# Normalisations and statistics of neighbouring batches moved to other heads of a batch in an attention and expert kernel

## The chip, the cores and the metric

The kernel runs on one core of a Trainium2 chip. Its time is that of one execution on the device, in microseconds. The engines are TensorE (PE, with its weight loads as PEld), VectorE (DVE), ScalarE (ACT), GpSimd (POOL) and SyncE (SP, which only issues transfers). Each runs its own list of instructions in order and waits on semaphores for the others.

## What is computed

Tokens of 8 batches of 512 are embedded (width 256), then go through a causal attention with 8 heads of width 128 and rotary positions, and through a layer of 8 experts. Cut to what matters, with `_layernorm(x) = (x - mean) / sqrt(var + 1e-5)`:

```python
h = jnp.take(weight, x, axis=0)
h = h + attention(_layernorm(h, axis=-1), w_aq, w_ak, w_av, w_ao)
h = h + experts(_layernorm(h, axis=-1), Wr, W1, b1, W2, b2)
```

```python
q, k, v = einsum('btm,mhd->bthd', x, w_a*)
s = einsum('bihd,bjhd->bhij', _rope(q), _rope(k)) / D_HEAD - 1e30 * (i < j)
r = einsum('bihd,hdm->bim', softmax(s) @ v, w_ao)
```

The first layernorm is needed ahead of a batch's first head. The second needs the output of the batch's last head, and its result is wanted only by the experts, after all batches.

## The kernel before

The attention stage takes the span up to some 746 us, the router and the experts the rest; the change touches the attention alone. All products are in fp32 split into a high and a low part: `x_hi` is made by ACT (L254), `x_lo` by DVE or POOL (L354, L218), and each product is three matmuls (L546).

The loop is written out by hand (`batches`, L107): for each batch `b`, eight slots, `h` = 0 to 7, and three more at the end of the last batch. Slot `h` does four heads at once in a pipeline, on every engine in a fixed order:

- head `h`: projections of q and k, the rotation, a block of the values;
- head `h-1`: scores in four row blocks (`minimum` on DVE L411, `exp` on ACT L272), and POOL's first three normalisations (`norm`, L198) at the end of the slot;
- head `h-2`: the last normalisation, transposes of the probabilities on TensorE in three fills (`turn`, L600), their high parts on ACT and low parts on DVE (`t_low`);
- head `h-3`: probabilities by values (`weigh`) and output projection (`output`).

POOL's order in a slot is: `q_sin` (L206, after DVE's `rope_q` L387 and ACT's swap L295), `q_cos` (L212), `norm` of head `h-2`'s last block, `k_cos` (L212), `qT_lo` and `kT_lo` (L218), then the extras of the slot, then `norm` of head `h-1` after DVE's `inverse` (L418), then further extras. ACT makes `qT_hi` after `q_cos`, then `exp 0`, then `v_hi`. DVE makes `rope_q`, `turn_k` (L395 to L397), `oT_lo`, `t_low 0`, `minimum 0, 1, 2`, extras, `v_lo`, extras, `t_low 1`, `minimum 3`, `t_low 2`, `inverse`, extras. TensorE starts a slot with the projection of q, which waits for the previous slot's last `v_lo`, since both use the bank `proj_ps[0]`; `turn 0` waits for two of the normalisations at the end of the slot before, `turn 1` for the last block's, `weigh` for `t_low 1` and, in its last part, for `t_low 2` of the slot before.

The extras are the work of neighbouring batches:

- for batch `b+1`: four gathers of embedding rows by POOL (`gather`, L171: block 0 in slot 3, block 1 in slot 4, blocks 2 and 3 in slot 5), `stats_of` (L360) and `aggregate` (L366) on DVE in slot 6, the root on POOL (`rsqrt`, L178 and L181) in slot 6 ahead of `norm`, `normalise` (L374) on DVE at the end of slot 6, the transposes `xt` (L555) on TensorE in slot 7, and their high and low parts `xT_hi`, `xT_lo`;
- for batch `b-1`: `evacuate` at the end of slot 2, `stats2_of` (L436) in slot 3, `aggregate2` (L443) at its end, the root `rsqrt2` (L187, L190) on POOL at the end of slot 4, and `normalise2` (L451) in slot 5, two blocks ahead of `v_lo` and two ahead of `t_low 1`.

In batch 0 there is no work for a batch before, in batch 7 none for a batch after.

Of the kernel before, what the change touches and what calls it, by code (L numbers as in the profile page):

```python
# [14 lines left out]
H, D = 8, 128  # L15
VOCAB = 8000
N = B * T
TB = T // P
# [20 lines left out]
def build_attention(nc, a, ident, h2, x2, wr, shared):  # L39
# [3 lines left out]
    with ctx:  # L43
# [117 lines left out]
        def _(pool):  # L161
# [3 lines left out]
            def gather(b, blocks):  # L165
                after(pool, "ids_in", (b + 1) * 16)
                after(pool, "res_in", b * 16)
                after(pool, "xn_ready", b)
                alone(pool)
                for tb in blocks:  # L170
                    pool.indirect_dma_start(emb[:, tb, :], None, a["emb"][:, :],  # L171
                                            bass.IndirectOffsetOnAxis(ids[:, tb:tb + 1], 0))\
                        .then_inc(s["emb_in"], 16)

            def rsqrt(b):
                after(pool, "aggr_done", b + 1)
                alone(pool)
                nc.gpsimd.tensor_scalar(rstd[:], mean_var[:, :, 1], EPS, None, ALU.add)\  # L178
                    .then_inc(s["var_eps"], 1)
                after(pool, "var_eps", b + 1)  # L180
                nc.gpsimd.tensor_tensor(rstd[:], rstd[:], neg_half[:], ALU.pow)\  # L181
                    .then_inc(s["rstd_done"], 1)
# [42 lines left out]
            def body(b, slots, ok):  # L225
                for h in slots:
                    n = b * H + h
                    live = ok(h) and h < H
                    if live:
                        add(b, h, "q")  # L230
                    if ok(h - 2):
                        after(pool, "inv_done", 2 * (n - 2) + 2)
                        norm(b, h - 2, [3])
                    if live:
                        add(b, h, "k")
                        low(b, h, "q")
                        low(b, h, "k")
                    if len(slots) == H and h in (3, 4, 5):
                        gather(b + 1, [h - 3])
                    if len(slots) == H and h == 6:  # L240
                        rsqrt(b + 1)
                    if ok(h - 1):
                        after(pool, "inv_done", 2 * (n - 1) + 1)
                        norm(b, h - 1, [0, 1, 2])
                    if len(slots) == H and h == 5:
                        gather(b + 1, [3])
                    if h == 4 and not (isinstance(b, int) and b == 0):
                        rsqrt2(b - 1)
            batches(pool, body)

        @block.scalar
# [100 lines left out]
        def _(dve):  # L352
# [13 lines left out]
                    last = nc.vector.bn_aggr(mean_var[:, tb, :], stats[:, tb, :])  # L366
                last.then_inc(s["aggr_done"], 1)

            def normalise(b):
                after(dve, "rstd_done", b + 1)  # L370
                after(dve, "h2_out", 16 * (b - 1))
                after(dve, "xt_tr", KT * b)
                for tb in range(TB):
                    last = nc.vector.tensor_scalar(xn[:, tb, :], emb[:, tb, :], mean_var[:, tb, 0:1],  # L374
                                                   rstd[:, tb:tb + 1], ALU.subtract, ALU.mult)
                last.then_inc(s["xn_ready"], 1)

            def xt(b):
                for kt in range(KT):
# [76 lines left out]
            def layernorm2(b, h, half):  # L456


                if isinstance(b, int) and b == 0 or h >= H:
                    return  # L460
                if h == 3:
                    stats2_of(b - 1, range(2 * half, 2 * half + 2))
                if h == 5:
                    normalise2(b - 1, range(2 * half, 2 * half + 2))

            dve.wait_ge(s["mask_ready"], 2)
            stats_of(0, range(TB))
            aggregate(0)
            normalise(0)
            after(dve, "w_hi", 1)  # L470
            low_of(w_qkv["q"][1][:], wraw["q"], w_qkv["q"][0][:], "w_lo")
            xt(0)
# [5 lines left out]
            def body(b, slots, ok):  # L478
                for h in slots:
# [14 lines left out]
                    if ok(h - 1):  # L494
# [3 lines left out]
                        after(dve, "s_done", 3 * (n - 1) + 2)  # L498
                        minimum(b, h - 1, 1)
                        minimum(b, h - 1, 2)  # L500
                    layernorm2(b, h, 0)
                    if len(slots) == H and h == 6:
                        stats_of(b + 1, [0, 1])
                    if live:
                        for i, t in enumerate(V_SLOT[h]):
                            after(dve, "v_hi", 2 * TB * b + t + 1)
                            low_of(v[1][:, t, :], proj_ps[i][:], v[0][:, t, :], "v_lo")
                    if isinstance(b, int) and b == 0 and h == 1:
                        after(dve, "w_hi", 4)
                        low_of(w_o[1][:], wraw_o, w_o[0][:], "w_lo")  # L510
                    if len(slots) == H and h == 7:
                        xt(b + 1)
                    layernorm2(b, h, 1)
                    if len(slots) == H and h == 6:
                        stats_of(b + 1, [2, 3])
                        aggregate(b + 1)
                    if ok(h - 2):
                        t_low(b, h - 2, 1)
                    if ok(h - 1):
                        after(dve, "s_done", 3 * (n - 1) + 3)  # L520
                        minimum(b, h - 1, 3)
# [8 lines left out]
                        aggregate2(b - 1)  # L530
                    if h == 10:
                        evacuate(b)
                    if len(slots) == H and h == 6:
                        normalise(b + 1)
            batches(dve, body)

        @block.tensor
# [921 lines left out]
```

## Time and profile before

| | before |
|---|---|
| median of 3 runs | 1239.88 us (1239.66 to 1241.63) |
| the profiled execution | 1239.33 us |
| its span, first to last instruction | 1237.4 us |
| PE busy | 1121.4 us (91%) |
| DVE busy | 830.0 us (67%) |
| POOL busy | 819.0 us (66%) |
| ACT busy | 692.1 us (56%) |
| mean granted clock of TensorE | 0.970 of full speed |

The page gives the busy time of each engine, and then shows the span in slices and the costliest groups. In a timeline a row is one instruction, or several alike that follow each other (x2, x3): its start from the beginning of the span, its length, engine, line, operation, the tiles (written <- read), and in brackets how long the engine was idle before it and what ended that. The tile `h` at L374 is `xn`, `x` at L451 is `x2`, and all PSUM tiles are called `bank`. A slot is here the stretch from TensorE's first matmul of one head's projection to that of the next.

### The profile page before, as it was taken

How to read it: one execution, taken by the hardware profiler on the slowest of the kernel's cores; microseconds unless marked ns; L12 is line 12 of the kernel's file. 1: busy time of each engine (PE TensorE's matmuls, PEld its weight loads, DVE VectorE, ACT ScalarE, POOL GpSimd, SP SyncE). 2: the span in 40 equal slices, each digit the busy share in tenths (PEclk: the TensorE clock that was granted, in tenths of full speed). 3: DMA queues.
4: the chain of work that ended last, by engine and by line, in shares of the span. 5: the costliest groups of instructions: out<-in, count | busy, mean ns of one | idle time of the engine just before them, and what ended most of it. 6: DMA issues, size and time to landing. Idle time of an engine off the chain costs nothing. (4 is left out here: it accounts for less than half of the span.)

```text
span 1237.4 us, 19984 instructions
## 1 busy us (share of the span) xinstructions
PE 1121.4 (91%) x6999; PEld 982.0 (79%) x6999; DVE 830.0 (67%) x1964; ACT 692.1 (56%) x1434; POOL 819.0 (66%) x886
## 2 busy tenths in 40 slices
PE   3899999999999999999999998117999999999997
PEld 2788888888888878878888874016999999999996
DVE  4777787887787787887887855774554555554433
ACT  3666666656656666666666654004554654655542
POOL 3797897887887888887987851014664654744534
PEclk9999999999999999999999999558999999999999
DMA  5000110110100100100100003302433523624223
GB/s 191 1 18 1 39 31 1 39 30 2 44 26 1 44 26 1 44 27 3 46 22 35 18 1 108 107 13 57 121 81 67 129 38 101 134 35 108 26 26 34
DMA packets 42211, 58.09 MB, mean 47 GB/s; under 512 B 8897, under 2 KB 34945, under 8 KB 41985
## 3 DMA queue, kind: packets, MB, share of 16 engines
q0 software_dynamic: 13824, 21.24, 9.8%
q1 hardware_dynamic: 28288, 35.58, 8.7%
q8 instruction: 56, 0.92, 0.3%
q14 instruction: 43, 0.34, 0.1%
HBM read 35.71 MB, written 16.91 MB: 43 GB/s over the span
## 5 line engine op out<-in xcount | busy, mean ns | idle before, releaser
L1098 DVE TENSOR_TENSOR hT_lo<-hid,hT_hi 128x512 fp32r<-128x512 f32 x124 | 86.4, 697 | 170.1 <-ACT hT_hi L1245 157.2
L198 POOL TENSOR_SCALAR prob<-prob,row_inv 128x512 f32<-128x512 f32 (+3 forms) x256 | 135.3, 541 | 69.1 <-DVE row_inv L418 67.4
L1242 ACT ACTIVATE hid<-up,b_e 128x512 f32<-128x512 f32 x128 | 88.1, 688 | 150.4 <-PE up L1345 136.1
L272 ACT ACTIVATE prob<-prob,row_min 128x512 f32<-128x512 f32 (+3 forms) x256 | 142.4, 556 | 40.1 <-DVE row_min L411 39.3
L867 POOL DMA_INDIRECT x<-routed_rows,tokens x64 | 84.3, 1318 | 112.7 <-DVE tokens L1092 95.0
L354 DVE TENSOR_TENSOR pT_lo<-bank,pT_hi 128x384 fp32r<-128x384 f32 (+1 forms) x192 | 114.3, 595 | 42.4 <-ACT pT_hi L254 42.4
L878 POOL TENSOR_SCALAR y<-y,gate 128x256 f32<-128x256 f32 x60 | 32.4, 552 | 128.0 <-issue 127.2
L411 DVE CUSTOM_DVE_ANT_0 prob<-bank,mask_row 128x512 f32<-128x512 f32 (+3 forms) x256 | 114.1, 483 | 0.0
L206 POOL TENSOR_TENSOR q_sin<-q_sin,rope_t 128x512 f32<-128x512 f32 x64 | 82.5, 1290 | 43.6 <-ACT q_sin L296 42.0
L887 POOL DMA_INDIRECT out<-y,tokens x60 | 97.2, 1621 | 16.1 <-issue 13.9
L600 PE MATMUL bank<-ident,prob 128*128 128x128 f32 x640 | 101.7, 273 | 5.6 <-POOL prob L198 5.6
L254 ACT ACTIVATE pT_hi<-bank 128x384 fp32r<-128x384 f32 (+1 forms) x192 | 99.5, 518 | 2.7 <-PE bank L600 2.5
L218 POOL TENSOR_TENSOR kT_lo<-k_cos,kT_hi 128x512 fp32r<-128x512 f32 x64 | 83.0, 1296 | 9.6 <-ACT kT_hi L254 9.2
L212 POOL TENSOR_TENSOR q_cos<-q_cos,q_sin 128x512 f32<-128x512 f32 x64 | 82.6, 1291 | 5.0
L600 PEld LDWEIGHTS bank<-ident,prob 128*128 128x128 f32 x640 | 76.7, 140 | 10.8 <-POOL prob L198 8.5
L546 PE MATMUL bank<-pT_hi,v_hi 128*128 128x512 f32 (+3 forms) x256 | 83.2, 325 | 1.9 <-DVE pT_lo L354 1.9
L1245 ACT ACTIVATE hT_hi<-up,b_e 128x512 fp32r<-128x512 f32 x124 | 84.7, 683 | 0.0
L546 PE MATMUL bank<-kT_hi,qT_hi 128*128 128x512 f32 (+3 forms) x256 | 84.5, 330 | 0.0
L218 POOL TENSOR_TENSOR qT_lo<-q_cos,qT_hi 128x512 fp32r<-128x512 f32 x64 | 83.3, 1301 | 0.0
L546 PE MATMUL bank<-pT_hi,v_lo 128*128 128x512 f32 (+3 forms) x256 | 83.0, 324 | 0.0
L212 POOL TENSOR_TENSOR k_cos<-k_cos,k_sin 128x512 f32<-128x512 f32 x64 | 82.9, 1295 | 0.0
L546 PE MATMUL bank<-kT_hi,qT_lo 128*128 128x512 f32 (+3 forms) x256 | 82.7, 323 | 0.0
(239 smaller groups left out, 3821.7 us busy)
## 6 DMA issues: line engine op xcount, KB each, us to landing
raw<-in_w SPq DMA_DIRECT2D x16, 1024.0 KB
emb_res<-emb SPq DMA_DIRECT2D x8, 512.0 KB, 3.7
out<-h SPq DMA_DIRECT2D x8, 512.0 KB, 2.9
routed_rows<-x SPq DMA_DIRECT2D x8, 512.0 KB, 3.1
x<-in_wq SPq DMA_DIRECT2D x1, 1024.0 KB, 5.1
x<-in_wk SPq DMA_DIRECT2D x1, 1024.0 KB, 4.9
x<-in_wv SPq DMA_DIRECT2D x1, 1024.0 KB, 7.0
x<-in_wo SPq DMA_DIRECT2D x1, 1024.0 KB, 10.1
```

Source lines behind the costliest of these rows:

```text
L198: nc.gpsimd.tensor_scalar(pr, pr, row_inv[:, h % 2, k:k + 1], 1.0, ALU.mult, ALU.mult).then_inc(s["norm_done"], 1)
L212: nc.gpsimd.tensor_tensor(cos[:], cos[:], sin[:], ALU.add).then_inc(s[f"{x}_add"], 1)
L218: nc.gpsimd.tensor_tensor(out[1][:, h % 2, :], cos[:], out[0][:, h % 2, :].bitcast(F32), ALU.subtract).then_inc(s[f"{x}_lo"], 1)
L254: nc.scalar.activation(out, in_, ACT.Copy).then_inc(s[name], 1)
L272: nc.scalar.activation(pr, pr, ACT.Exp, bias=row_min[:, h % 2, k:k + 1], scale=-1.0, accum_out=row_sum[:, h % 2, k:k + 1]).then_inc(s["exp ...
L354: nc.vector.tensor_tensor(out, in_, hi.bitcast(F32), ALU.subtract)\
L411: nc.vector.tensor_tensor_reduce(prob[:, h % 2, col:col + w], s_ps[bk][:, pc:pc + w], mask_row[:, T - w:T], scale=-1.0 / D, scalar=3e38, o ...
L546: last = nc.tensor.matmul(out, l, r, start=start and c == 0, stop=stop and c == len(todo) - 1)
L600: last = nc.tensor.transpose(t_ps[f][:, c * P:(c + 1) * P], prob[:, h % 2, col:col + P], ident[:])
L887: pool.indirect_dma_start(a["out"][:, :], bass.IndirectOffsetOnAxis(tokens[e][:, TB * half + c:TB * half + c + 1], 0), y[half][:, c, :], N ...
L1098: nc.vector.tensor_tensor(out, in_, hi.bitcast(F32), ALU.subtract)\
L1242: nc.scalar.activation(hid[:, t % 2, :], up_ps[t % 2][:], ACT.Gelu, bias=bias)
```

## The change

- POOL: the gathers of blocks 0 and 1 stand in slot 3, those of blocks 2 and 3 in slot 4; none is left in slot 5. `rsqrt2(b - 1)` stands at the end of slot 3 instead of slot 4, and `rsqrt(b + 1)` at the end of slot 5 instead of in slot 6 ahead of `norm`.
- DVE: `v_lo` now stands ahead of the first half of the extras, and `t_low 1` ahead of the second half. `normalise2` is in slot 4 instead of 5; `stats_of` and `aggregate` are in slot 5 instead of 6; `normalise` takes a list of blocks and is cut in two halves within slot 6, in place of one piece at its end.
- No instruction is added or dropped, and no buffer changes.

```diff
--- before.py
+++ after.py
@@ -235,17 +235,15 @@
                         add(b, h, "k")
                         low(b, h, "q")
                         low(b, h, "k")
-                    if len(slots) == H and h in (3, 4, 5):
-                        gather(b + 1, [h - 3])
-                    if len(slots) == H and h == 6:
-                        rsqrt(b + 1)
+                    if len(slots) == H and h in (3, 4):
+                        gather(b + 1, [2 * h - 6, 2 * h - 5])
                     if ok(h - 1):
                         after(pool, "inv_done", 2 * (n - 1) + 1)
                         norm(b, h - 1, [0, 1, 2])
+                    if h == 3 and not (isinstance(b, int) and b == 0):
+                        rsqrt2(b - 1)
                     if len(slots) == H and h == 5:
-                        gather(b + 1, [3])
-                    if h == 4 and not (isinstance(b, int) and b == 0):
-                        rsqrt2(b - 1)
+                        rsqrt(b + 1)
             batches(pool, body)
 
         @block.scalar
@@ -366,14 +364,15 @@
                     last = nc.vector.bn_aggr(mean_var[:, tb, :], stats[:, tb, :])
                 last.then_inc(s["aggr_done"], 1)
 
-            def normalise(b):
+            def normalise(b, blocks):
                 after(dve, "rstd_done", b + 1)
                 after(dve, "h2_out", 16 * (b - 1))
                 after(dve, "xt_tr", KT * b)
-                for tb in range(TB):
+                for tb in blocks:
                     last = nc.vector.tensor_scalar(xn[:, tb, :], emb[:, tb, :], mean_var[:, tb, 0:1],
                                                    rstd[:, tb:tb + 1], ALU.subtract, ALU.mult)
-                last.then_inc(s["xn_ready"], 1)
+                if TB - 1 in blocks:
+                    last.then_inc(s["xn_ready"], 1)
 
             def xt(b):
                 for kt in range(KT):
@@ -460,13 +459,13 @@
                     return
                 if h == 3:
                     stats2_of(b - 1, range(2 * half, 2 * half + 2))
-                if h == 5:
+                if h == 4:
                     normalise2(b - 1, range(2 * half, 2 * half + 2))
 
             dve.wait_ge(s["mask_ready"], 2)
             stats_of(0, range(TB))
             aggregate(0)
-            normalise(0)
+            normalise(0, range(TB))
             after(dve, "w_hi", 1)
             low_of(w_qkv["q"][1][:], wraw["q"], w_qkv["q"][0][:], "w_lo")
             xt(0)
@@ -498,24 +497,28 @@
                         after(dve, "s_done", 3 * (n - 1) + 2)
                         minimum(b, h - 1, 1)
                         minimum(b, h - 1, 2)
-                    layernorm2(b, h, 0)
-                    if len(slots) == H and h == 6:
-                        stats_of(b + 1, [0, 1])
                     if live:
                         for i, t in enumerate(V_SLOT[h]):
                             after(dve, "v_hi", 2 * TB * b + t + 1)
                             low_of(v[1][:, t, :], proj_ps[i][:], v[0][:, t, :], "v_lo")
+                    layernorm2(b, h, 0)
+                    if len(slots) == H and h == 5:
+                        stats_of(b + 1, [0, 1])
+                    if len(slots) == H and h == 6:
+                        normalise(b + 1, [0, 1])
                     if isinstance(b, int) and b == 0 and h == 1:
                         after(dve, "w_hi", 4)
                         low_of(w_o[1][:], wraw_o, w_o[0][:], "w_lo")
                     if len(slots) == H and h == 7:
                         xt(b + 1)
+                    if ok(h - 2):
+                        t_low(b, h - 2, 1)
                     layernorm2(b, h, 1)
-                    if len(slots) == H and h == 6:
+                    if len(slots) == H and h == 5:
                         stats_of(b + 1, [2, 3])
                         aggregate(b + 1)
-                    if ok(h - 2):
-                        t_low(b, h - 2, 1)
+                    if len(slots) == H and h == 6:
+                        normalise(b + 1, [2, 3])
                     if ok(h - 1):
                         after(dve, "s_done", 3 * (n - 1) + 3)
                         minimum(b, h - 1, 3)
@@ -530,8 +533,6 @@
                         aggregate2(b - 1)
                     if h == 10:
                         evacuate(b)
-                    if len(slots) == H and h == 6:
-                        normalise(b + 1)
             batches(dve, body)
 
         @block.tensor
```

## Rows read from the trace of the kernel before

**Rows 1.** Busy time by stretch, slots 4 to 7 (length, engines' busy us, clock).

```profile
237.36:247.91 10.55, 10.55 (x68) 9.45 (x66) 7.74 (x25) 7.48 (x19) 10.16 (x11) 1.00 0.05 12
247.91:259.33 11.42, 10.79 (x67) 9.45 (x65) 10.18 (x22) 7.44 (x20) 10.70 (x13) 1.00 0.05 13
259.33:270.13 10.80, 10.80 (x65) 9.45 (x65) 9.04 (x24) 5.76 (x14) 9.43 (x11) 1.00 0.27 73
270.13:283.01 12.88, 11.12 (x68) 9.26 (x67) 10.83 (x30) 7.56 (x19) 10.48 (x13) 1.00 0.01 2
```

**Rows 2.** Timeline of TensorE, slots 5 to 7 (start, us, line, [idle before]).

```profile
252.70 0.49 PE L600 MATMUL bank<-ident,prob 128*128 128x128 f32 x3
...
259.33 0.50 PE L546 MATMUL bank<-xT_hi,wq_hi 128*128 128x512 f32 x1 [0.63 <-DVE v_lo L354]
...
280.29 0.66 PE L600 MATMUL bank<-ident,prob 128*128 128x128 f32 x4 [0.67 <-POOL prob L198]
...
283.01 0.50 PE L546 MATMUL bank<-xT_hi,wq_hi 128*128 128x512 f32 x1 [0.67 <-DVE xT_lo L354]
```

**Rows 3.** Waits, batches 1 to 6 (total us, times, longest).

```profile
PE bank L546 <- DVE v_lo L354: 3.8, 6, 0.6
```

**Rows 4.** Timeline of POOL, end of slot 3 to slot 5.

```profile
238.51 1.09 POOL L171 DMA_INDIRECT emb<-in_emb,ids  x1 [0.16 <-issue]
...
239.65 1.61 POOL L198 TENSOR_SCALAR prob<-prob,row_inv 128x512 f32<-128x512 f32 x3
...
241.37 1.29 POOL L206 TENSOR_TENSOR q_sin<-q_sin,rope_t 128x512 f32<-128x512 f32 x1
...
249.67 1.60 POOL L198 TENSOR_SCALAR prob<-prob,row_inv 128x512 f32<-128x512 f32 x3 [0.24 <-DVE row_inv L418]
...
252.74 1.29 POOL L206 TENSOR_TENSOR q_sin<-q_sin,rope_t 128x512 f32<-128x512 f32 x1
```

**Rows 5.** Timeline of POOL, kernel's start and batch 3's slot 3 (two pieces).

```profile
7.49 0.95 POOL L171 DMA_INDIRECT emb<-in_emb,ids  x1 [0.30 <-issue]
...
328.85 1.26 POOL L198 TENSOR_SCALAR prob<-prob,row_inv 128x512 f32<-128x512 f32 x2
```

**Rows 6.** Timelines, slot 6: the chain behind q_sin.

```profile
264.84 1.29 POOL L206 TENSOR_TENSOR q_sin<-q_sin,rope_t 128x512 f32<-128x512 f32 x1
...
269.38 0.69 DVE L354 TENSOR_TENSOR v_lo<-bank,v_hi 128x512 fp32r<-128x512 f32 x1 [1.27 <-ACT v_hi L254]
...
270.39 0.58 ACT L254 ACTIVATE pT_hi<-bank 128x512 fp32r<-128x512 f32 x1
```

**Rows 7.** Timelines, slots 5 and 6: normalisations and their company.

```profile
255.90 2.77 DVE L451 TENSOR_SCALAR x<-h,mean_var,rstd 128x256 f32<-128x256 f32 x2
...
257.19 1.34 POOL L218 TENSOR_TENSOR qT_lo<-q_cos,qT_hi 128x512 fp32r<-128x512 f32 x1
...
259.20 1.10 DVE L451 TENSOR_SCALAR x<-h,mean_var,rstd 128x256 f32<-128x256 f32 x2
...
273.21 2.02 DVE L374 TENSOR_SCALAR h<-emb,mean_var,rstd 128x256 f32<-128x256 f32 x4 [0.49 <-POOL rstd L181]
```

**Rows 8.** Timelines, ends of slots 5 and 6: statistics, t_low, inverse.

```profile
260.23 0.68 DVE L354 TENSOR_TENSOR pT_lo<-bank,pT_hi 128x512 fp32r<-128x512 f32 x1
...
261.64 0.16 DVE L418 RECIPROCAL row_inv<-row_sum 128x3 f32<-128x3 f32 x1
...
262.01 1.61 POOL L198 TENSOR_SCALAR prob<-prob,row_inv 128x512 f32<-128x512 f32 x3 [0.94 <-DVE row_inv L418]
...
269.99 0.74 DVE L360 BATCH_NORM_STATS2 stats<-emb 128x6 f32<-128x256 f32 x2
...
271.18 0.66 DVE L354 TENSOR_TENSOR pT_lo<-bank,pT_hi 128x512 fp32r<-128x512 f32 x1
```

**Rows 9.** Timelines, slot 7: rope_q and q_sin of head 7.

```profile
275.15 0.67 DVE L387 TENSOR_TENSOR q_cos<-bank,rope_t 128x512 f32<-128x512 f32 x1
...
277.14 1.28 POOL L206 TENSOR_TENSOR q_sin<-q_sin,rope_t 128x512 f32<-128x512 f32 x1 [2.05 <-ACT q_sin L296]
```

## The prediction

> **What bounds the kernel now.** I read four views in this order. First the busy times by stretch, cut where TensorE starts the projection of a new head (I call such a stretch a slot; batch 2 starts at 193.81 us) [rows 1]. In slot 4 TensorE is busy for all of its 10.55 us and DVE, ACT and POOL are not, so TensorE sets the pace; the clock is 1.00 throughout. Slots 5, 6 and 7 last 11.42, 10.80 and 12.88 us. Their matmuls are those of slot 4 (slot 7 has transposes of about the same length in place of one set of values), so 0.87 + 0.25 + about 2.3 = 3.4 us per batch is all that a better order could return, about 24 us over seven batches. Second, TensorE's own rows with a wait [rows 2]: slot 6 starts late because `v_lo` of slot 5 came late, slot 7's `turn 1` waits for POOL's `prob`, and slot 0 of the next batch waits for `xT_lo`. The first of these happens once in each of the batches 1 to 6 [rows 3]. Third, POOL and then DVE in order of time [rows 4, 6, 7, 8], because each of these late tiles comes out of POOL's or DVE's hand-written queue.
>
> The relation that I use most: POOL's `q_sin` of a head feeds `q_cos`, then ACT makes `qT_hi`, the first exponential and `v_hi`, and DVE makes `v_lo`, for which the next slot's projection waits. In slot 6 nothing in that chain waits for anything else: `q_sin` starts at 264.84, `v_lo` at 269.38 (4.54 later), and slot 7 at 270.13, **5.29 us after `q_sin`** [rows 1, 6]. So a slot keeps its 10.55 us only if `q_sin` starts by 10.55 - 5.29 = 5.26 us into it. Today head 4's starts at 241.37, which is 4.01 in, and head 5's, behind a gather and the root, at 252.74, 4.83 in [rows 4]. POOL has under 1.3 us to spare in slot 4.
>
> **The change part by part, in batch 2.**
>
> *Slot 3, POOL.* A second gather and `rsqrt2` now stand ahead of head 4's `q_sin`. A gather directly behind another costs 0.30 of issue and 0.95 of work, 1.25 [rows 5]. The normalisation starts at 239.65 right behind the one gather [rows 4], so it moves to 240.90. From the normalisation to `q_sin` with a root between it takes 252.74 - 249.67 = 3.07 [rows 4]. `q_sin` of head 4 then starts at 243.97, 6.61 into slot 4, and slot 5 starts at 243.97 + 5.29 = 249.26. Slot 4 becomes 11.90: **+1.35**. What was covered in slot 3 by spare time is no longer covered. DVE's statistics of slot 3 move behind `v_lo` and `t_low 1` and delay its next `rope_q` by a pair of statistics, 0.75 [rows 8]; that is hidden, since POOL is not ready for its result.
>
> *Slot 4, POOL and DVE.* From `q_sin` at 241.37 to the end of one gather POOL needs 8.06 (the normalisation at 249.67 has 0.24 of idle time before it) [rows 4]; with a second gather it is free at 243.97 + 8.06 + 1.25 = 253.3. On DVE `v_lo` starts at 243.97 + 4.54 = 248.5, and the pair of `normalise2` behind it meets POOL's two long subtractions. Such a pair took 2.77 beside them, and a pair that met only the tail of one took 1.10 [rows 7]; held until 251.0, and with 1.41 from `t_low 1` to the inverse [rows 8] and 0.66 for the other pair DVE reaches the inverse at 253.1. (0.66 is an estimate for a pair with no POOL instruction beside it; by the four of slot 6 it would be 2.02 / 2 = 1.01 [rows 7].) Inverse to normalisation takes 262.01 - 261.64 = 0.37 [rows 8]. Both ways the normalisation begins at 253.4 and its first two pieces take 1.26 [rows 5], to 254.66. TensorE wants them 252.70 - 247.91 = 4.79 into slot 5 [rows 1, 2], at 254.05: a new stall of 0.61.
>
> *Slot 5.* It loses the `normalise2` pair ahead of `v_lo`, its 0.87 stall, and two gathers. It gains the 0.61. The next `q_sin` is at 253.1 + 0.08 + 1.99 = 255.1 (1.99 from `rope_q` to `q_sin`, as [rows 9] have it), which permits slot 6 at 260.4; the stall gives 249.26 + 10.55 + 0.61 = 260.42. Slot 5 becomes 11.16: **-0.26**.
>
> *End of slot 5.* `t_hi 1` on ACT ends 6.13 after `q_sin` (264.84 to 270.39 + 0.58) [rows 6], at 261.2. DVE then needs 261.64 - 260.23 = 1.41 to the inverse, and for the moved second pair of statistics and the aggregate 271.18 - 269.99 = 1.19 more [rows 8]. So the inverse is at 263.8, POOL's normalisation at 264.18, and with the root now behind it and ahead of `q_sin`, head 6's `q_sin` starts at 264.18 + 3.07 = 267.25. Slot 7 starts at 267.25 + 5.29 = 272.54. Slot 6 becomes 12.12 instead of 10.80: **+1.32**. Before, this root stood ahead of the normalisation, in time in which POOL would have waited for the inverse anyway.
>
> *Slot 6 and 7.* The four pieces of `normalise` leave the end of slot 6, where they took 2.02 with POOL in its own short pieces [rows 7], after a wait of 0.49. Two of them now follow `v_lo`, at 271.79 + 0.60 = 272.39. POOL's `qT_lo` and `kT_lo` then run from 271.6 to 274.1 (POOL's order behind `q_sin` is fixed). In slot 5 of today the first pair of `normalise2` met two POOL instructions of this length, the later of them `qT_lo`, and ended just behind it (255.90 + 2.77 = 258.67 against 257.19 + 1.34 = 258.53) [rows 7]; so I let this pair hold DVE until 274.2; that is the only operation of the new place which the trace does not show. Its bounds are 0.66 and 2.77; the nearest row is the one with such partners; counted from 272.39, in the middle of the first, it gives 1.8. With the same 1.41 and 0.66 as in slot 4 and 0.08 to the next instruction, `rope_q` of head 7 starts at 276.35. From there to `q_sin` it took 277.14 - 275.15 = 1.99, and from `q_sin` to the next batch 283.01 - 277.14 = 5.87 [rows 2, 9]: 276.35 + 1.99 + 5.87 = 284.21. Slot 7 becomes 11.67 instead of 12.88: **-1.21**. The stalls at `prob` and `xT_lo` shrink because head 7's `q_sin` begins 5.8 and not 7.0 into its slot.
>
> **Sum.** 1.35 - 0.26 + 1.32 - 1.21 = +1.20 per batch, six times: 7.2. Batch 0 has no second layernorm, so no root in slot 3 and no stall in slot 4; but slot 6 and 7 follow from the same chain, and I count it as 1.2 too. Batch 7 has no gathers; the root alone sets `q_sin` of head 4 back, and after the gain in slot 5 I count 0.4. Together 8.8 us. The stage after the attention keeps its work and order: 0. The profiled execution took 1239.33 (span 1237.4), 0.55 under the median 1239.88. 1239.33 + 8.8 = 1248.1, by the median 1248.7; I say 1248.5.
>
> One rule of the Trainium skill bears on the term for the pair. In slot 5 two `TENSOR_SCALAR` of DVE took 2.77, while four of the same size took 2.02 at the end of slot 6 [rows 7]. "SBUF — State Buffer", section "Who interferes with whom", says that a DVE tensor_scalar in a two-port mode and a GpSimd instruction exclude each other for the whole instruction, whoever starts first; the trace agrees (1.4 for one, where POOL's took 1.3). By that rule both moves of normalisations, which put them directly behind `v_lo`, are into POOL's two subtractions. Without it the sum would be that of the second rival below.
>
> **Rivals.**
> (1) *The POOL backlog is absorbed, and the kernel gets faster.* If the gather and root in slot 3 cost POOL less than 1.4 of their 2.6 us, `q_sin` of head 4 stays within 5.26 and neither the 1.35 nor the 0.61 appears: 1.20 - 1.96 = -0.76 per batch, -5.3, and 1234.6. For it: slot 5 today bears a gather and a root. Against it: that `q_sin` starts already 4.83 in, with one item fewer. 12%.
> (2) *The pair in slot 6 isn't held.* Then it takes 0.66, `t_low 1` waits for ACT at 273.4 and `q_sin` of head 7 comes 0.8 earlier: +0.4 per batch, 1243. Against it: rows 7. 10%.
> (3) *No effect*: the moved instructions fit on all engines, and TensorE stays as it is. Against it are the 4.01 and 5.26 above. 5%, 1240.
> (4) *Slower still.* In slot 4 `t_low 1` ends only about 0.5, `t_low 2` about 0.3 ahead of TensorE's `weigh` in slot 5. If a further piece of `normalise2` meets a POOL instruction (some 1.4), `weigh` stalls by about 1 there, and slot 7 shifts likewise by a few tenths: 1.4 more per batch, 1258. 13%.
>
> **How the numbers follow.** The forecast has the remaining 60%, with its own range 1244 to 1254 (a quarter to three quarters of a microsecond per batch in either direction, from several maxima in a row). The range of 80% reaches over (2) and into (3) and (4): 1240 to 1257. A measurement tells about 0.2% (2.5 us) from no change. Faster: rival 1, 12%. Within 0.2%: rival 3 and half of 2, 10%. Slower: 78%.
>
> **What would show it.** Right: slot 4 of about 11.9 in batches 1 to 6, ended by `v_lo`; a wait of `turn 0` on `prob` in slot 5; slot 6 about 12.1, again ended by `v_lo`; slot 7 about 11.7; `q_sin` of heads 4 and 6 at 6.6 to 6.8 into their slots; the first pair of L374 at about 1.8 us in slot 6. Wrong: slot 4 still at 10.55, which would leave only the gains; or a TensorE wait on `pT_lo` in slots 5 or 7, which is rival 4.

## The result, and the profile after

The changed kernel takes 1249.61 us (median of 4 runs, 1249.22 to 1250.64) against 1239.91 before; the ratio is 1.0077, 95% interval 1.0059 to 1.0094. It is **slower by 9.7 us**; 1248.5 was forecast, in 1240 to 1257. The profiled execution took 1249.77 (span 1247.6, before 1237.4). TensorE's mean granted clock is 0.970 in both.

The busy time by stretch, slots 4 to 7 of batch 2 of the changed kernel (columns as in rows 1), where slot 4 begins at 239.94:

```profile
239.94:251.82 11.88, 11.06 (x68) 9.39 (x66) 8.31 (x26) 6.32 (x16) 11.03 (x13) 1.00 0.08 22
251.82:263.25 11.43, 10.77 (x65) 9.39 (x65) 10.06 (x25) 7.30 (x19) 10.83 (x12) 1.00 0.24 70
263.25:275.20 11.95, 11.12 (x68) 9.40 (x66) 8.79 (x28) 6.72 (x18) 9.39 (x12) 1.00 0.00 1
275.20:287.01 11.81, 10.54 (x68) 9.12 (x67) 10.39 (x24) 7.68 (x19) 9.16 (x11) 1.00 0.01 1
```

Against rows 1 slot 4 is longer by 1.33, slot 5 by 0.01, slot 6 by 1.15, and slot 7 is shorter by 1.07: +1.42 in this batch by rows 1's borders. From its start to the next batch's a batch takes 90.67 where it took 89.20 to 89.31 before. TensorE's waits over batches 1 to 6 (as rows 3) have another owner. In the kernel before, beside the row of rows 3:

```profile
PE bank L600 <- POOL prob L198: 4.0, 6, 0.7
```

In the changed kernel:

```profile
PE bank L601 <- POOL prob L198: 17.4, 24, 0.8
```

The wait for `v_lo` of rows 3 is no longer in the list, and the 6 waits for POOL's normalisations, at `turn 1` of slot 7, have become 24, one in each of the slots 4 to 7. TensorE's timeline shows them at `turn 1` (x4) or `turn 0` (x3), and the end of slot 4 at `turn 2`:

```profile
249.82 0.66 PE L601 MATMUL bank<-ident,prob 128*128 128x128 f32 x4 [0.82 <-POOL prob L198]
...
251.37 0.49 PE L601 MATMUL bank<-ident,prob 128*128 128x128 f32 x3
251.82 0.50 PE L547 MATMUL bank<-xT_hi,wq_hi 128*128 128x512 f32 x1
...
257.44 0.55 PE L601 MATMUL bank<-ident,prob 128*128 128x128 f32 x3 [0.66 <-POOL prob L198]
...
273.20 0.66 PE L601 MATMUL bank<-ident,prob 128*128 128x128 f32 x4 [0.83 <-POOL prob L198]
...
280.75 0.55 PE L601 MATMUL bank<-ident,prob 128*128 128x128 f32 x3 [0.59 <-POOL prob L198]
```

POOL's timeline from slot 3 on (as rows 4, 6 and 9):

```profile
241.06 1.09 POOL L171 DMA_INDIRECT emb<-in_emb,ids  x1 [0.15 <-issue]
...
242.46 0.97 POOL L171 DMA_INDIRECT emb<-in_emb,ids  x1 [0.31 <-DVE row_inv L417]
...
243.47 1.61 POOL L198 TENSOR_SCALAR prob<-prob,row_inv 128x512 f32<-128x512 f32 x3
...
246.54 1.29 POOL L206 TENSOR_TENSOR q_sin<-q_sin,rope_t 128x512 f32<-128x512 f32 x1
...
256.13 1.61 POOL L198 TENSOR_SCALAR prob<-prob,row_inv 128x512 f32<-128x512 f32 x3
...
266.84 1.61 POOL L198 TENSOR_SCALAR prob<-prob,row_inv 128x512 f32<-128x512 f32 x3 [2.22 <-DVE row_inv L417]
...
269.91 1.29 POOL L206 TENSOR_TENSOR q_sin<-q_sin,rope_t 128x512 f32<-128x512 f32 x1
```

From 241.06 to the `q_sin` at 246.54 there are two gathers, a normalisation and a root with no idle time of more than 0.31, and `q_sin` of head 4 starts 6.60 into slot 4. `q_sin` of head 6, at 269.91, has the root of the next batch ahead of it and starts 6.66 into slot 6. The next slots begin 5.28 and 5.29 later, at 251.82 and 275.20. DVE's timeline (as rows 7 and 8) shows the two normalisations and, at the end of slot 5, the statistics in their new places:

```profile
251.07 0.69 DVE L352 TENSOR_TENSOR v_lo<-bank,v_hi 128x512 fp32r<-128x512 f32 x1 [3.06 <-ACT v_hi L252]
...
251.68 2.04 DVE L450 TENSOR_SCALAR x<-h,mean_var,rstd 128x256 f32<-128x256 f32 x2
...
254.24 0.72 DVE L450 TENSOR_SCALAR x<-h,mean_var,rstd 128x256 f32<-128x256 f32 x2
...
263.89 0.69 DVE L352 TENSOR_TENSOR pT_lo<-bank,pT_hi 128x512 fp32r<-128x512 f32 x1 [0.26 <-ACT pT_hi L252]
264.50 0.74 DVE L358 BATCH_NORM_STATS2 stats<-emb 128x6 f32<-128x256 f32 x2
...
266.47 0.17 DVE L417 RECIPROCAL row_inv<-row_sum 128x3 f32<-128x3 f32 x1
...
274.45 0.69 DVE L352 TENSOR_TENSOR v_lo<-bank,v_hi 128x512 fp32r<-128x512 f32 x1 [2.70 <-ACT v_hi L252]
...
275.06 2.04 DVE L372 TENSOR_SCALAR h<-emb,mean_var,rstd 128x256 f32<-128x256 f32 x2
...
277.62 0.72 DVE L372 TENSOR_SCALAR h<-emb,mean_var,rstd 128x256 f32<-128x256 f32 x2
```

In both places the first pair, directly behind `v_lo`, takes 2.04 and the second 0.72. Ahead of `v_lo` DVE was idle for 3.06 and 2.70. The second pair of statistics and the aggregate stand behind `t_low 1` (263.89) and ahead of the inverse (266.47).

### The profile page after: what moved, and what is told of

It reads as the page before. It is cut to its first block and busy times, and to the rows that moved or that the text cites. A ratio compares the mean times of both kernels' runs of the same rounds, so it can differ in the third digit from the quotient of the medians.

```text
span 1247.6 us, 19963 instructions
## 1 busy us (share of the span) xinstructions
PE 1123.8 (90%) x6999; PEld 979.7 (79%) x6999; DVE 824.1 (66%) x1964; ACT 690.3 (55%) x1434; POOL 817.9 (66%) x886
## 5 line engine op out<-in xcount | busy, mean ns | idle before, releaser
L352 DVE TENSOR_TENSOR v_lo<-bank,v_hi 128x512 fp32r<-128x512 f32 x64 | 44.2, 692 | 89.9 <-ACT v_hi L252 89.9
L601 PEld LDWEIGHTS bank<-ident,prob 128*128 128x128 f32 x640 | 73.7, 140 | 34.7 <-POOL prob L198 32.9
L252 ACT ACTIVATE qT_hi<-q_cos 128x512 fp32r<-128x512 f32 x64 | 40.4, 632 | 103.8 <-POOL q_cos L212 103.8
```

The source lines that it names most:

```text
L252: nc.scalar.activation(out, in_, ACT.Copy).then_inc(s[name], 1)
L352: nc.vector.tensor_tensor(out, in_, hi.bitcast(F32), ALU.subtract)\
L601: last = nc.tensor.transpose(t_ps[f][:, c * P:(c + 1) * P], prob[:, h % 2, col:col + P], ident[:])
```

## Experiments: one part of the change at a time

The theory is that of the prediction, in short the **queue theory**: a slot begins 5.29 after POOL's `q_sin` of the slot before or at its own 10.55, whichever is later; POOL's work ahead of `q_sin`, and DVE's work ahead of the inverse, decide. The rivals are that DVE's pieces held by POOL cost the time wherever they stand (held pieces), that it is the place of the root and not the amount of POOL's work (place), and that DVE's new order with `v_lo` first helps.

**The work for the batch before, alone.** On the kernel before:

```diff
-                    if h == 4 and not (isinstance(b, int) and b == 0):
+                    if h == 3 and not (isinstance(b, int) and b == 0):
                         rsqrt2(b - 1)
...
-                if h == 5:
+                if h == 4:
                     normalise2(b - 1, range(2 * half, 2 * half + 2))
```

> The kernel before with one part of the change alone: rsqrt2 at the end of slot 3 and normalise2 in slot 4. The queue theory (a slot starts 5.29 us after POOL's q_sin of the slot before, or at its 10.55) gives: one root, 1.5 us, comes ahead of head 4's q_sin, which then starts 5.4 into slot 4 (limit 5.26): slot 4 at 10.6 to 10.7. Slot 5 has neither the root nor a normalise2 pair ahead of v_lo: 10.6. Everything behind it keeps its distances, so 0.7 us less per batch in batches 1 to 6 and some 0.4 in batch 7: 1235. The rival that it is DVE's pieces held by POOL's long instructions that cost, wherever they stand, expects no gain from the move: 1240. The rival that moving a root ahead of q_sin is what spoiled slot 4 expects the loss of 1.3 of slot 4 in full: 1247.

Measured: 1236.47 against 1240.49 before on the same chip, ratio 0.9966 (0.9956 to 0.9976). It is faster than both kernels. Slots 4 and 5 of batch 2, by stretch:

```profile
237.74:248.33 10.59, 10.59 (x68) 9.45 (x66) 8.51 (x26) 6.15 (x16) 10.03 (x12) 1.00 0.05 12
248.33:259.22 10.89, 10.78 (x66) 9.38 (x65) 9.31 (x21) 7.38 (x19) 9.97 (x11) 1.00 0.20 62
```

Slot 4 is at 10.59, so a root alone in slot 3 does not spoil it: `q_sin` starts there 5.31 into the slot, at the limit. Slot 5 is at 10.89 and not at 10.6, because `turn 0` waits for a normalisation and starts 5.08 into the slot instead of 4.79: the second pair of `normalise2` took 2.20, beside POOL's two subtractions, and POOL waited 0.59 for the inverse behind it. So the gain is 0.55 per batch instead of 0.7. Both rivals expected a worse time.

**The gathers alone.** On the kernel before:

```diff
-                    if len(slots) == H and h in (3, 4, 5):
-                        gather(b + 1, [h - 3])
+                    if len(slots) == H and h in (3, 4):
+                        gather(b + 1, [2 * h - 6, 2 * h - 5])
...
-                    if len(slots) == H and h == 5:
-                        gather(b + 1, [3])
```

> The kernel before with the gathers alone moved (0 and 1 in slot 3, 2 and 3 in slot 4). Queue theory: head 4's q_sin starts 4.01 + 1.27 = 5.3 into slot 4, so slot 4 stays at 10.55 to 10.6; in slot 4 two gathers and the root stand ahead of head 5's q_sin, which comes 7.1 into slot 5: slot 5 at 12.4 instead of 11.42; then slots 6 and 7 keep their relation to it with two gathers fewer in slot 5: +0.5 per batch in batches 1 to 6, none in batch 0: 1243. Rival, DVE's held pieces: no change, 1240.

Measured: 1245.69 (1242.92 to 1245.93) against 1240.49, ratio 1.0038 (1.0023 to 1.0052). By stretch:

```profile
239.07:249.74 10.67, 10.67 (x68) 9.38 (x66) 7.70 (x23) 6.59 (x17) 10.08 (x11) 1.00 0.09 25
249.74:261.93 12.19, 11.14 (x68) 9.38 (x65) 9.15 (x22) 6.81 (x18) 11.36 (x14) 1.00 0.08 23
```

A second gather in slot 3 leaves slot 4 near its 10.55; the second gather in slot 4, with the root, makes slot 5 12.19 (12.4 was expected). A batch is 0.7 longer where 0.5 was expected. The pairs of `normalise2` stand where they stood, and the time moved. The median is 2.7 above the 1243 that was expected.

**DVE's order alone.** On the kernel before:

```diff
-                    layernorm2(b, h, 0)
-                    if len(slots) == H and h == 6:
-                        stats_of(b + 1, [0, 1])
                     if live:
                         for i, t in enumerate(V_SLOT[h]):
                             after(dve, "v_hi", 2 * TB * b + t + 1)
                             low_of(v[1][:, t, :], proj_ps[i][:], v[0][:, t, :], "v_lo")
+                    layernorm2(b, h, 0)
+                    if len(slots) == H and h == 6:
+                        stats_of(b + 1, [0, 1])
...
+                    if ok(h - 2):
+                        t_low(b, h - 2, 1)
                     layernorm2(b, h, 1)
                     if len(slots) == H and h == 6:
                         stats_of(b + 1, [2, 3])
                         aggregate(b + 1)
-                    if ok(h - 2):
-                        t_low(b, h - 2, 1)
```

> The kernel before with DVE's new order alone (v_lo ahead of the extras' first half, t_low 1 ahead of the second), all else as before. Queue theory: slot 5 loses its wait for v_lo (10.55), but the inverse at its end comes 0.35 later, so head 6's q_sin and slot 7 come 0.4 later than before the edit (slot 6 at 12.0), and in slot 6 the statistics behind t_low 1 delay the root, DVE waits for it, and rope_q of slot 7 comes 1.35 later: +1.35 per batch, 1249. Rival (v_lo first takes a stall from TensorE and costs nothing): 0.9 to 1.1 less per batch, 1233.

Measured: 1253.69 against 1239.14 on its chip, ratio 1.0118 (1.0101 to 1.0135), the slowest of all runs. Slots 5, 6 and 7 of batch 2:

```profile
252.39:262.94 10.55, 10.55 (x67) 9.44 (x66) 7.52 (x20) 6.36 (x16) 10.04 (x12) 1.00 0.05 14
262.94:275.28 12.34, 11.22 (x68) 9.39 (x66) 9.82 (x24) 7.05 (x18) 10.67 (x12) 1.00 0.20 64
275.28:289.41 14.13, 11.31 (x67) 9.16 (x67) 11.68 (x32) 7.54 (x19) 10.46 (x13) 1.00 0.01 2
```

As both theories said, slot 5 loses its wait; as the queue theory said, slots 6 and 7 give back more. The size was off: 1.9 per batch and not 1.35. Slots 5 and 6 together are 0.67 longer and slot 7 is 1.25 longer. The rows of DVE and POOL show where it arises:

```profile
262.17 0.69 DVE L354 TENSOR_TENSOR v_lo<-bank,v_hi 128x512 fp32r<-128x512 f32 x1 [1.71 <-ACT v_hi L254]
...
262.78 2.04 DVE L451 TENSOR_SCALAR x<-h,mean_var,rstd 128x256 f32<-128x256 f32 x2
```

```profile
278.20 0.24 POOL L178 TENSOR_SCALAR rstd<-mean_var 128x4 f32<-128x4 f32 x1 [1.35 <-DVE mean_var L366]
```

The 1.25 of slot 7 is not due to held pieces: the four of `normalise` take 2.00 where they took 2.02. It is the statistics and the aggregate behind `t_low 1` of slot 6, for which POOL's root now waits 1.35; it starts 2.92 into slot 7 instead of 1.67, and `rope_q` 6.26 instead of 5.02. Of the 0.67, some 0.4 are there already at head 5's `q_sin` (15.80 behind the start of slot 4, before 15.38), where the only new thing on DVE is the second pair of slot 3's statistics behind `t_low 1`: by it the inverse comes 2.32 into slot 4 instead of 1.68, and with it `rope_q` and head 4's `q_sin`, at 4.64 instead of 4.01. The last 0.26 lie between head 5's `q_sin` and the inverse (9.16 against 8.90), where the first pair of `normalise2` is held for 2.04 behind `v_lo`. TensorE's waits for `prob` come to 15.7 us in 24 waits here, with no root and no gather moved.

**The changed kernel with DVE's order of before** (the reverse of the last edit, on the changed kernel):

```diff
-                    if live:
-                        for i, t in enumerate(V_SLOT[h]):
-                            after(dve, "v_hi", 2 * TB * b + t + 1)
-                            low_of(v[1][:, t, :], proj_ps[i][:], v[0][:, t, :], "v_lo")
                     layernorm2(b, h, 0)
...
                     if len(slots) == H and h == 6:
                         normalise(b + 1, [0, 1])
+                    if live:
+                        for i, t in enumerate(V_SLOT[h]):
+                            after(dve, "v_hi", 2 * TB * b + t + 1)
+                            low_of(v[1][:, t, :], proj_ps[i][:], v[0][:, t, :], "v_lo")
...
-                    if ok(h - 2):
-                        t_low(b, h - 2, 1)
                     layernorm2(b, h, 1)
...
                     if len(slots) == H and h == 6:
                         normalise(b + 1, [2, 3])
+                    if ok(h - 2):
+                        t_low(b, h - 2, 1)
```

> The changed kernel with DVE's order of before: the extras' first half ahead of v_lo, the second half ahead of t_low 1. In the changed kernel DVE idles 3.06 us ahead of v_lo in slot 4 and 2.70 in slot 6; the first pair now fits in there. Queue theory: slot 4 keeps 11.9 and slot 5 11.4 (POOL's queue sets both), but the inverse at the end of slot 5 comes 1.0 earlier and with it head 6's q_sin, and slot 7's rope_q another 0.6: slot 6 at 11.0, slot 7 at 11.2, 1.6 less per batch, over seven batches 11: 1239. Rival (v_lo first is a help, since a late v_lo stalls TensorE): slots 4 and 6 longer by the pair, 1255 or more. Rival (POOL alone matters): 1249.6.

Measured: 1239.46 against 1240.49, ratio 0.9996 (0.9987 to 1.0006). **With DVE's old order all the loss is gone**, although POOL's moves are all there:

```profile
238.76:250.69 11.93, 10.94 (x67) 9.39 (x65) 9.48 (x27) 6.21 (x16) 11.09 (x13) 1.00 0.08 22
250.69:262.27 11.58, 10.75 (x66) 9.34 (x65) 10.35 (x25) 7.57 (x20) 10.99 (x12) 1.00 0.24 69
262.27:273.20 10.93, 10.80 (x68) 9.46 (x66) 8.82 (x28) 6.56 (x18) 9.38 (x12) 1.00 0.00 1
273.20:284.52 11.32, 10.55 (x68) 9.10 (x66) 9.90 (x22) 7.82 (x20) 9.32 (x11) 1.00 0.01 1
```

Slots 4 and 5 stay near those of the changed kernel (11.93 and 11.58 against 11.88 and 11.43), as POOL's queue has it; slots 6 and 7 are at 10.93 and 11.32 instead of 11.95 and 11.81. Against the kernel before the moves still cost 1.38 in slot 4 and 0.16 and 0.13 in slots 5 and 6, and slot 7, at 11.32 instead of 12.88, gives back 1.56: batch 2 takes 89.30 where it took 89.20. DVE's timeline shows the first pairs in the time in which DVE would have waited for `v_hi`:

```profile
246.75 1.79 DVE L450 TENSOR_SCALAR x<-h,mean_var,rstd 128x256 f32<-128x256 f32 x2
...
249.95 0.69 DVE L352 TENSOR_TENSOR v_lo<-bank,v_hi 128x512 fp32r<-128x512 f32 x1 [1.41 <-ACT v_hi L252]
...
250.56 2.21 DVE L450 TENSOR_SCALAR x<-h,mean_var,rstd 128x256 f32<-128x256 f32 x2
...
263.09 0.66 DVE L352 TENSOR_TENSOR pT_lo<-bank,pT_hi 128x512 fp32r<-128x512 f32 x1
...
264.47 0.16 DVE L417 RECIPROCAL row_inv<-row_sum 128x3 f32<-128x3 f32 x1
...
270.27 0.77 DVE L372 TENSOR_SCALAR h<-emb,mean_var,rstd 128x256 f32<-128x256 f32 x2
...
272.45 0.69 DVE L352 TENSOR_TENSOR v_lo<-bank,v_hi 128x512 fp32r<-128x512 f32 x1 [1.42 <-ACT v_hi L252]
...
273.06 2.20 DVE L372 TENSOR_SCALAR h<-emb,mean_var,rstd 128x256 f32<-128x256 f32 x2
```

The pair at 246.75 is held for 1.79, and `v_lo` still has 1.41 of idle time before it: a held piece costs next to nothing there.

The same rows show what DVE's order costs in the changed kernel, and that it is not the holding. The pair directly behind `v_lo` is held in both orders, for 2.04 with the new one and for 2.20 with the old. In slot 5 the new order puts the second pair of statistics and the aggregate between `t_low 1` and the inverse: 2.58 from one to the other (266.47 - 263.89) against 1.38 with the old order (264.47 - 263.09). `t_low 1` itself begins 0.19 earlier, counted from head 5's `q_sin`, so the inverse comes 8.72 after that (266.47 - 257.75) and not 7.71 (264.47 - 256.76). That is the 1.02 of slot 6. In slot 6 it puts one pair of `normalise` behind `t_low 1` that the old order does in the idle time ahead of `v_lo`: 0.64 more there, less the 0.17 by which the held pair is shorter, nearly the 0.49 of slot 7.

## Experiments: amount, place and the held piece

**The changed kernel with 1.5 us less on POOL.** The second layernorm's root is computed once, for batch 0, and used for all (this leaves work out and alters the second layernorm's scale):

```diff
-                    if h == 3 and not (isinstance(b, int) and b == 0):
+                    if h == 3 and b == 1:
                         rsqrt2(b - 1)
...
-                after(dve, "rstd2_done", b + 1)
+                after(dve, "rstd2_done", 1)
```

> The changed kernel with the root of the second layernorm left out from batch 2 on (it is computed once, for batch 0, and used again, so the second layernorm's scale is another). 1.5 us of POOL per batch is gone from the end of slot 3, nothing else. Queue theory: head 4's q_sin 5.1 into slot 4, slot 4 at 10.55 in batches 2 to 6 (11.88 in the changed kernel), turn 0 of slot 5 still waits 0.7, and every later slot comes 1.47 earlier: 5 x 1.47 + 0.4 = 7.8 less than the changed kernel's 1249.6, 1241.8. Rival, DVE's held pairs of 2.04 us in slots 4 and 6 set the time: they are all still there, so 1249.6.

Measured: 1242.77 against 1240.49, ratio 1.0018 (1.0008 to 1.0027). Slots 4 and 5:

```profile
239.83:250.49 10.66, 10.66 (x68) 9.39 (x66) 8.57 (x26) 6.61 (x18) 10.07 (x11) 1.00 0.09 25
250.49:261.64 11.15, 10.73 (x67) 9.37 (x66) 9.77 (x24) 6.80 (x17) 10.28 (x12) 1.00 0.23 72
```

A batch takes 89.23 here and 90.64 in batch 1 of the same run, which still has its root: 1.4 for 1.5 us of POOL. DVE's pairs are all there, so holding them does not by itself set the time.

**The same root at another place.** In the changed kernel it goes into slot 4, behind `k_cos`:

```diff
                     if live:
                         add(b, h, "k")
+                    if h == 4 and not (isinstance(b, int) and b == 0):
+                        rsqrt2(b - 1)
+                    if live:
                         low(b, h, "q")
...
-                    if h == 3 and not (isinstance(b, int) and b == 0):
-                        rsqrt2(b - 1)
```

> The changed kernel with rsqrt2 taken from the end of slot 3 and put into slot 4, between k_cos and qT_lo, where it delays only the low parts. The amount of POOL's work ahead of head 5's q_sin is the same as before the edit, only its place is another. Queue theory (POOL has no idle time from slot 3's gathers to head 5's q_sin, so the amount counts): head 4's q_sin 5.1 into slot 4, slot 4 at 10.6, but slot 5 at 12.7, and the sum of both as in the changed kernel (23.3): 1249.6 within 1.5. Rival (the place counts: the root spoiled slot 4 because it stood ahead of q_sin): slot 4 at 10.6, slot 5 stays at 11.4, 1.3 less per batch: 1241.5.

Measured: 1251.41 against 1239.14, ratio 1.0096 (1.0079 to 1.0113).

```profile
241.46:252.09 10.63, 10.63 (x67) 9.37 (x66) 8.26 (x25) 6.58 (x17) 9.87 (x12) 1.00 0.08 25
252.09:264.70 12.61, 11.06 (x67) 9.35 (x66) 10.88 (x25) 6.96 (x19) 11.98 (x13) 1.00 0.25 64
```

The stall moved from slot 4 to slot 5, and the sum is 23.24, in the changed kernel 23.31. The place rival falls. TensorE also waits 0.68 for `pT_lo` in slot 5 here, since the pair of `normalise2`, which waits for the root, took 2.70; the later wait of `turn 0` for POOL's normalisation (0.87) covers it.

A batch takes 90.57 here, 0.1 less than in the changed kernel, but the median is 1.8 above it, a little more than the 1.5 that was allowed. The profiled execution was 1.7 longer in batch 0: slot 0 lasted 12.23 at a granted clock of 0.86 (in the changed kernel 11.34 at 1.00), slot 2 11.69 at 0.85 (10.85 at 0.84). The profiled executions of the kernel with DVE's old order and of the cut in two and two, below, have the same two longer slots, so they do not come from this edit; why slot 2 is longer at nearly the same clock is open.

**One more edit on the kernel before: `normalise` behind `rope_q` of slot 7.** Slot 7 was the longest slot before, and in it `rope_q` waited for the root and four pieces.

```diff
+                    if len(slots) == H and h == 7:
+                        normalise(b + 1)
                     if live:
                         turn_k(b, h)
...
-                    if len(slots) == H and h == 6:
-                        normalise(b + 1)
```

> The kernel before with one edit that is not in the change: normalise stands behind rope_q and the single inverse of slot 7 instead of ahead of them at the end of slot 6. Queue theory: rope_q of head 7 starts 2.5 earlier, ACT's swap is ready before POOL's normalisations end, q_sin of head 7 starts some 2.0 earlier, and then minimum 0 of slot 7 (0.67 earlier) and the exponential behind it set xT_hi and xT_lo: slot 7 at 11.6 instead of 12.88, 1.3 less in each of seven batches: 1231. Rival (slot 7 is bound by TensorE's wait for xn, or by normalise itself): 1240 or more, since xn is no earlier.

Measured: 1239.60 against 1239.14, ratio 1.0004 (0.9994 to 1.0014): no change, a miss by 8 us. The DVE rows and the POOL row of slot 7:

```profile
273.16 3.07 DVE L374 TENSOR_SCALAR h<-emb,mean_var,rstd 128x256 f32<-128x256 f32 x4
```

```profile
274.77 1.32 POOL L206 TENSOR_TENSOR q_sin<-q_sin,rope_t 128x512 f32<-128x512 f32 x1
```

`q_sin` did come earlier, 4.8 into the slot instead of 7.0, but then the fourth piece of `normalise`, begun at 274.87, met it and lasted 1.37 where it had lasted 0.46; the four took 3.07 instead of 2.02. `turn_k` came 0.46 later into the slot for it (276.15 - 270.00 against 275.82 - 270.13), and slot 7 stayed at 12.74. The edit freed POOL, and POOL's freed instruction stood in DVE's way.

**Both edits**, the first and the last:

> The kernel before with the edits of the runs that move rsqrt2 to slot 3 and normalise2 to slot 4, and normalise behind rope_q of slot 7. The first gave 0.55 per batch in slot 5. They act on slots with no common wait, so the gains should add: 1231 - 4 = 1227. If slot 6 and 7 give the first gain back, 1231.

Measured: 1235.67 against 1239.14, ratio 0.9968 (0.9956 to 0.9979): the gain of the first alone. 1227 was expected with the last edit's forecast gain, which isn't there.

**The held piece avoided.** If that reading is right, it must help to cut `normalise` so that all its pieces are over when `q_sin` starts. On the kernel with the first edit (`normalise` takes a list of blocks here, as in the change):

```diff
+                    if len(slots) == H and h == 7:
+                        normalise(b + 1, [2, 3])
                     if live:
                         turn_k(b, h)
...
                     if len(slots) == H and h == 6:
-                        normalise(b + 1)
+                        normalise(b + 1, [0, 1])
```

> The kernel before with rsqrt2 and normalise2 moved as in the change, and normalise cut: blocks 0 and 1 at the end of slot 6, blocks 2 and 3 behind rope_q and the single inverse of slot 7. In the run with all four behind rope_q the fourth piece met POOL's q_sin, which had come earlier, and took 1.37 instead of 0.46. Theory (DVE's piece waits for POOL's running instruction, and q_sin follows rope_q by 1.99): rope_q starts 1.0 earlier than at present, the last two pieces lie in front of q_sin, turn_k starts 0.3 earlier, and both ways into the exponential of slot 7 end some 0.9 earlier: slot 7 at 11.95 instead of 12.87, 0.9 less in seven batches, 6.5 less than the 1236.5 of the two moves: 1230. Rival (what costs is normalise standing ahead of turn_k, wherever it is cut): slot 7 at 12.75, 1235.7.

Measured: 1229.79 against 1240.36, ratio 0.9910 (0.9894 to 0.9927). Slot 7 and DVE's rows in it:

```profile
269.00:280.93 11.93, 10.95 (x67) 9.21 (x66) 10.63 (x30) 7.57 (x19) 10.46 (x13) 1.00 0.01 2
```

```profile
272.08 1.05 DVE L374 TENSOR_SCALAR h<-emb,mean_var,rstd 128x256 f32<-128x256 f32 x2 [0.24 <-POOL rstd L181]
...
273.71 0.71 DVE L374 TENSOR_SCALAR h<-emb,mean_var,rstd 128x256 f32<-128x256 f32 x2
```

The four pieces take 1.05 and 0.71, POOL's `q_sin` starts at 275.04, behind them, and slot 7 is at 11.93 (11.95 expected).

**The cut at one and three**, with `[0]` and `[1, 2, 3]` in the same two places:

> As the cut in two and two, but block 0 at the end of slot 6 and blocks 1 to 3 behind rope_q and the single inverse. rope_q starts 0.6 earlier still, and q_sin would follow at 275.5 in the times of batch 2, just as the last piece begins. Theory: if the last piece begins first, slot 7 is that of the cut in two and two (minimum 0 sets it) within 0.1, 1230; if it meets q_sin, it is held by 1.3 and slot 7 is 12.7 or more, 1236. Rival (the held piece has nothing to do with q_sin's start): the same time as with all four behind rope_q, 1235.7, in both cuts.

Measured: 1228.66 against 1240.36, ratio 0.9907 (0.9890 to 0.9923), slot 7 at 11.87. The last piece took 0.40 and lay in front of `q_sin`. The two cuts can't be told apart: a batch takes 87.6 to 87.8 in both. They are the fastest of all kernels, 20 and 21 us under the changed one.

## Why the prediction was right

The point and all its signs held, one of them narrowly (slot 4 ended by `v_lo`); term by term, for a batch of 1 to 6:

- *Slot 4, +1.35 predicted, +1.33 measured.* `q_sin` of head 4 was put 6.61 into the slot and came at 6.60; 5.29 from there to the next slot was 5.28. The two gathers took 2.41 to the normalisation (243.47 - 241.06), 1.14 + 1.25 = 2.39 in the sum. What I had not seen is that `turn 1` waits there too, for the last block's normalisation, which follows `q_sin`. `v_lo` comes still later, but only by 0.20: the projection starts 0.45 after `turn 2` (251.82 - 251.37), where it took 0.25 in the kernel before (247.91 - 247.66, rows 1 and the row below). Without the wait for `v_lo` slot 4 would still be some 1.13 longer (an estimate: 1.33 - 0.20). Both ways start from the same `q_sin`, so the term holds.

```profile
247.66 0.49 PE L600 MATMUL bank<-ident,prob 128*128 128x128 f32 x3
```

- *Slot 5, -0.26 predicted, +0.01 measured.* `turn 0` waited as forecast (257.44), but for 0.83 over its place and not 0.61: POOL came to the normalisation 9.59 after `q_sin` (256.13 - 246.54), and the sum had 9.4. This is the largest miss of a term.
- *Slot 6, +1.32 predicted, +1.15 measured.* The inverse, the 0.37 behind it (266.84 - 266.47), the root and `q_sin` stand as in the sum; the chain runs from head 5's `q_sin`, so the end of slot 6 stayed where it was, while its start came later by what slot 5 was longer. Slots 5 and 6 together: +1.06 predicted, +1.16 measured.
- *Slot 7, -1.21 predicted, -1.07 measured.* The first pair held DVE for 1.96 to the next instruction (277.02 - 275.06) and not 1.8.
- *Batch 0, +1.2 predicted*, 86.76 against 85.55: +1.21, which is luck. The prediction gave no working for it, and its own terms for slots 6 and 7 add up to 0.11. What came was +0.21 in slot 5, +1.38 in slot 6 and only -0.40 in slot 7, which had lasted 12.22 in batch 0 and not 12.88. *Batch 7, +0.4 predicted*: slot 4 at 11.01, +0.46.
- *Sum: 8.8 predicted; the span grew by 10.2, the medians by 9.7.* The rest is 0.2 to 0.3 per batch, times six: slots 5 and 7 came out 0.41 above their terms, slots 4 and 6 0.19 below.

Of the rivals, number 1 (POOL's backlog absorbed) is refuted by slot 4 at 11.88 and by the root left out: 1.5 us of POOL were worth 1.4 of a batch. Number 2 (the pair is not held) is refuted by the 2.04. Number 3 (no effect) is refuted by the 9.7 us. Number 4 did not occur in the changed kernel: TensorE has no wait for `pT_lo`. With the root in slot 4 it did, for 0.68.

One reading that the prediction invites has to be corrected by the runs. It gave each slot its own cause and never priced DVE's new order by itself, though the statistics behind `t_low 1` stand in its sum for slot 6. The runs show **that the whole loss comes from the order**: all the moves with DVE's old order 1239.5, as before; DVE's new order with everything else in its old place 1253.7; both 1249.6. So the moves cost nothing with the old order (slot 4 pays, slot 7 gives back) and save 4 to 5 us with the new one, while the new order costs 10 us in the changed kernel and 14.5 in the kernel before. It does so by putting DVE's extras behind `v_lo` and `t_low 1`, ahead of the inverse on which POOL's next `q_sin` depends, instead of into time in which DVE waits. In the changed kernel these are the statistics (1.0 per batch, in slot 6) and one pair of `normalise` that nothing holds (0.5, in slot 7); in the kernel before, by the rows above, at least 1.6 of the 1.9 per batch are statistics. The pieces that POOL holds are real, and with `normalise` in slot 7 they decided the time, but they are hardly what the order costs. These shares are read from the traces; no run moved the statistics alone.

## What to carry to other kernels

Where TensorE is busy all the time in most stages, look for the one instruction of a helper engine from which the next stage's start has a fixed distance, and count what stands ahead of it in its queue; work for a neighbour may be moved only up to that slack, here 1.25 us in slot 4. Put such extras into time in which the engine would wait anyway (ahead of the late operand), not behind the wait, even if the operand behind them looks urgent. And when an edit makes an engine's instruction come earlier, ask beside which instruction of another engine it now falls.

## What the runs showed of the hardware

- A DVE `TENSOR_SCALAR` of 128x256 in SBUF took 0.40 to 0.42 with POOL idle or gathering. One that met a POOL `TENSOR_TENSOR` of 128x512 (1.29) took up to 1.49, and in nearly all cases of the 12 traces it ended 0.15 after POOL's instruction (0.26 at most). The same instruction went from 0.46 to 1.37 when an edit that touched neither put `q_sin` beside it. The Trainium skill, "SBUF — State Buffer", section "Who interferes with whom", describes this, for a DVE `tensor_scalar` in a two-port mode, as exclusion for the whole instruction; the traces agree, though they do not show the mode.
- Two gathers issued one behind the other by POOL kept it for 2.41 us to the next instruction, one alone for 1.14; the second of them brought 0.31 of idle time with it.
